# Context keys and values of layer 1 moved into the first phase of a two-layer gated attention kernel

## What is computed

```python
# layer 1, attention; context is an input, latents = layernorm(x) after layer 0
kv = jnp.concatenate([context, latents], axis=1)
q = (latents @ Wq).reshape(bsz, q_len, HEADS, HEAD_DIM).transpose(0, 2, 1, 3)
k = (kv @ Wk).reshape(bsz, kv_len, KV_HEADS, HEAD_DIM).transpose(0, 2, 1, 3)
v = (kv @ Wv).reshape(bsz, kv_len, KV_HEADS, HEAD_DIM).transpose(0, 2, 1, 3)
q, k = rms_norm(q, q_norm_w), rms_norm(k, k_norm_w)
qg = q.reshape(bsz, KV_HEADS, groups, q_len, HEAD_DIM)
probs = softmax(einsum('bhgqd,bhkd->bhgqk', qg, k) * scale)
out = einsum('bhgqk,bhkd->bhgqd', probs, v) ... @ Wo
# layer 0: k = context @ w_k.T, v = context @ w_v.T, 32 heads; codes of the
# feed-forward: idx = sum over planes p of ((qweight[p] >> shift) & 1) << p
```

## Time and profile before

| | us |
|---|---|
| median of 3 runs | 1750.46 (1750.33 to 1751.2) |
| the profiled execution | 1750.49 |
| its span, first to last instruction | 1748.7 |
| outside the span | 1.8 |
| PE busy | 1701.0 (97%) |
| PE weight loads busy | 1540.4 (88%) |
| DVE busy | 1146.8 (66%) |
| ACT busy | 856.4 (49%) |
| POOL busy | 554.3 (32%) |
| mean granted clock of PE | 0.991 |

### The profile page before, as it was taken

How to read it: one execution, slowest core, us unless ns; L and a number is a source line. 1 busy time by engine, 2 the same in 40 slices (tenths; PEclk the granted TensorE clock), 3 DMA queues, 4 the chain that set the end, 5 groups by cost and what they waited for, 6 DMA issues and landing times.

```text
span 1748.7 us, 31125 instructions
## 1 busy us (share of the span) xinstructions
PE 1701.0 (97%) x11031; PEld 1540.4 (88%) x11031; DVE 1146.8 (66%) x2064; ACT 856.4 (49%) x2254; POOL 554.3 (32%) x530
## 2 busy tenths in 40 slices
PE   6999999989999999999889999999999999999998
PEld 5999999978999999999768989898998989898987
DVE  7334443788777777778987566675756666565576
ACT  4333434444445454454425555555555555555553
POOL 4232222253222222222343333233333333232243
PEclk8999999999999999999989999999999999999999
DMA  5343434532333233332201001000100101010001
GB/s 219 146 168 144 168 144 161 184 120 84 113 105 107 94 106 112 105 105 70 88 16 37 25 25 37 12 25 22 36 24 24 36 12 42 6 36 15 1 1 48
DMA packets 62346, 132.29 MB, mean 76 GB/s; under 512 B 5200, under 2 KB 40400, under 8 KB 59216
## 3 DMA queue, kind: packets, MB, share of 16 engines
q1 hardware_dynamic: 62288, 131.52, 22.0%
HBM read 95.85 MB, written 35.65 MB: 75 GB/s over the span
## 4 chain that ended last, share of the span: by engine, by line
PE 90%; DVE 6%; ACT 1%; issue 1%; POOL 1%; DMA 0%; SPq 0%; DVEq 0%; POOLq 0%
PE bank L1611 20%; PE bank L1613 20%; PE bank L1612 19%; PE bank L1659 17%; PE bank L1955 3%; PE bank L1805 3%; PE bank L1762 3%; PE bank L1974 2%; PE bank L1750 1%; PE bank L1853 1%; PE bank L1979 1%; DVE stats L1004 1%; DVE vw_lo L1035 0%; POOL residual L562 0%; PE bank L1628 0%
## 5 line engine op out<-in xcount | busy, mean ns | idle before, releaser
L623 POOL TENSOR_TENSOR p<-p,rn 128x512 f32<-128x512 f32 x128 | 131.2, 1046 | 244.5 <-DVE rn L1487 244.5
L565 POOL TENSOR_TENSOR pr<-pr,rn 128x512 f32<-128x512 f32 x64 | 66.7, 1042 | 369.2 <-DVE rn L1234 369.2
L1611 PE MATMUL bank<-w_hi,xt_hi 128*128 (+2 forms) x512 | 177.6, 347 | 0.0
L1613 PE MATMUL bank<-w_hi,xt_lo 128*128 (+2 forms) x512 | 172.5, 337 | 0.0
L1612 PE MATMUL bank<-w_lo,xt_hi 128*128 (+2 forms) x512 | 171.3, 335 | 0.0
L1611 PE MATMUL bank<-xt_hi,w0q_hi 128*128 128x256 f32 x512 | 149.4, 292 | 0.0
L919 ACT ACTIVATE p<-bank,nb,q_r 128x256 f32<-128x256 f32 x256 | 141.3, 563 | 11.5 <-DVE nb L1483 4.8
L1612 PE MATMUL bank<-xt_lo,w0q_hi 128*128 128x256 f32 x512 | 144.0, 281 | 0.0
L1613 PE MATMUL bank<-xt_hi,w0q_lo 128*128 128x256 f32 x512 | 143.9, 281 | 0.0
L494 POOL TENSOR_TENSOR q_r<-q_ms,half 128x4 f32<-128x4 f32 x64 | 64.5, 1008 | 210.1 <-DVE q_ms L1463 210.1
L826 ACT ACTIVATE ptr<-bank 128x512 f32<-128x512 f32 x63 | 37.7, 598 | 185.9 <-PE bank L1750 185.9
(11 more groups left out here) (225 smaller groups left out, 5547.7 us busy)
## 6 DMA issues: line engine op xcount, KB each, us to landing
stage<-w SPq DMA_DIRECT2D x35, 512.0 KB, 3.3
keys_of_layer<-kout SPq DMA_DIRECT2D x16, 1024.0 KB, 4.3
values_of_layer<-vout SPq DMA_DIRECT2D x16, 1024.0 KB, 4.8
kt<-keys_of_layer SPq DMA_DIRECT2D x64, 256.0 KB, 3.1
vs<-values_of_layer SPq DMA_DIRECT2D x64, 256.0 KB, 2.8
kraw<-wk SPq DMA_DIRECT2D x16, 512.0 KB, 5.2
vraw<-wv SPq DMA_DIRECT2D x8, 1024.0 KB, 6.7
stage0q<-w SPq DMA_DIRECT2D x16, 512.0 KB, 3.8
```

Of the source, the lines that this page charges most:

```text
L565: pool.tensor_tensor(by4(pr), by4(pr), rn[:, :].unsqueeze(2).to_broadcast([P, 4, P]), ALU.mult).then_inc(norm_done, 1)
L623: pool.tensor_tensor(p1[:, half_p:half_p + 2, :], p1[:, half_p:half_p + 2, :], rn1[:, half_p:half_p + 2].unsqueeze(2).to_broadcast([P, 2, ...
L1611: nc.tensor.matmul(out_ap, l_hi, r_hi, start=(c == 0), stop=False)
L1613: op = nc.tensor.matmul(out_ap, l_lo, r_hi, start=False, stop=(c == n - 1))
```

## The change

1. In the first phase, after the eight groups of layer 0, four groups (`EG = KV // 2`) of two jobs each (k = 4, 5) make the context's keys and values of layer 1 for all 8 key/value heads by the same Strassen scheme, with the machinery of the values jobs; they are stored to DRAM (`kv1d`). Their weight sums are on DVE (`value_sums`), except those of the first group.
2. In layer 1, `keys_values` makes the latents' tile alone. The context's tile comes by DMA into a small double buffer (`kvc`), and `kv_out`, `v_low` and `k_scaled` read it there.
3. The weight codes are unpacked on DVE in the first two context groups in place of slots 1 to 7 of layer 0; `dequantise` runs once in every slot from the first on.
4. Rows of x are normalised and transposed during the context groups in place of the last group of layer 0.
5. The values' weight is split in three pieces (EARLY, MIDDLE, LAST) in place of two, and the order of the first operations differs: POOL's sums wait until three differences have been split, ACT's first evacuation of a values job comes ahead of the fourth difference.
6. `fbias` is loaded and scaled after layer 0; SP issues its DMA after the last `dequantise` and ahead of the five loads of layer 1's first weights.

```diff
         @block.sync
+            def store_context(e, half_s):
+                all_quarters(number(e, 4 + half_s))
+                for m in range(2):
+                    sp.dma_start(kv1d[2 * e + m, :, :, :]..., values_out(4 + half_s)[:, :, :, m, :])...
...
+            sp.wait_ge(wl_done, C * 2 ** LO_BITS)
+            sp.dma_start(fbias[:, :], ffn0_bias.to_broadcast([P, D])).then_inc(fbias_in, 16)
             for piece, used, count in ((2, w_lo_done[1], NG), (0, q_ps, U - 4), (1, y_ps, U - 4), (3, added, U), (4, s_ps, U)):
...
+            def load_context(t, j, held=True):
+                if held:
+                    sp.wait_ge(k1_scaled, BODY * t + j - 1)
+                sp.dma_start(kvc[:, j % 2, :], kv1d[t, :, j, :]).then_inc(kvc_in[j % 2], 16)
...
         @block.gpsimd
             weight_sums(vraw, vraw_in, vsum_done, 0, 0)
+            pool.wait_ge(t_lo_done, 7)
...
         @block.scalar
-            values_early(0)
+            values_weight(0, EARLY, 2)
             difference_hi(T2)
             first_keys(0, 0)
             first_keys(0, 1)
+            values_weight(0, MIDDLE, 5)
             difference_hi(T3)
             difference_hi(T1)
-            values_late(0)
-            difference_hi(T4)
             first_keys(1, 0)
             first_keys(1, 1)
...
+            def kv_out(count, place, loads):
                 for tile in range(2):
+                    if tile == 0:
+                        act.wait_ge(kvc_in[place % 2], 16 * loads)
+                    else:
+                        act.wait_ge(kv1_ps, count)
+                    nc.scalar.activation(v_hi[:, place, tile, :], key_value(tile, place)[:, P:2 * P], ACT.Copy)
+                    last_op = nc.scalar.activation(k_sq[:, tile, :], key_value(tile, place)[:, 0:P], ACT.Square,
                                                    accum_out=k_ss[:, tile:tile + 1])
...
         @block.vector
+            def context_projections(e):
+                values_weight_lo(SG + e, MIDDLE)
+                quarter11(e, 4)
+                quarter21(*((e - 1, 5) if e else (SG - 1, 3)))
+                values_weight_lo(SG + e, LAST)
+                quarter22(e, 4)
+                if e == 0:
+                    quantising_constants()
+                    unpack(0, "shift")
+                if e == 1:
+                    unpack(2, "shift")
+                if e == 2:
                     row_stats(0, 0)
                     row_stats(0, 1)
...
+                quarter11(e, 5)
+                quarter21(e, 4)
+                if e < EG - 1:
+                    value_sums(SG + e + 1)
+                    values_weight_lo(SG + e + 1, EARLY)
...
+                quarter22(e, 5)
+                if e == 0:
+                    unpack(0, "mask add")
+                    unpack(1, "shift mask add")
+                if e == 1:
+                    unpack(2, "mask add")
+                    unpack(3, "shift mask add")
+                if e == EG - 2:
+                    dve.wait_ge(lnw_in, 16)
+                    for b in range(3):
+                        normed_rows(0, b)
+                    row_stats(0, 2)
+                    row_stats(0, 3)
...
+                if first and j == 0:
+                    dve.wait_ge(vd_out, 16 * NG + 32 * EG)
+                    link(nc.vector.memset(wl[:, :, :], 0.0))
+                dequantise(2 * t + j // 4, j % 4, i + 1)
...
             def v_low(count, place):
                 dve.wait_ge(k1_squared, count)
+                for tile in range(2):
+                    last_op = nc.vector.tensor_tensor(v_lo[:, place, tile, :], key_value(tile, place)[:, P:2 * P],
+                                                      v_hi[:, place, tile, :].bitcast(fp32), ALU.subtract)
+                last_op.then_inc(v1_lo_done, 1)
...
         @block.tensor
+            def context_projections(e):
+                for k in (4, 5):
+                    products_early(e, k)
+                    products_last(*((e, 4) if k == 5 else (e - 1, 5) if e else (SG - 1, 3)))
+                    products_middle(e, k)
...
             def keys_values(b, parity, count):
                 wait(pe, kt1_lo_done, count - 1)
                 wait(pe, v1_lo_done, count - 1)
-                for tile, (xh, xl) in enumerate(((ct_hi, ct_lo), (xt_hi, xt_lo))):
-                    op = passes(by2(KVB[:, :])[:, tile, :],
-                                [(xh[:, c, tok(b)], xl[:, c, tok(b)], w1_hi[:, parity, 256 * c:256 * (c + 1)],
-                                  w1_lo[:, parity, 256 * c:256 * (c + 1)]) for c in range(C)])
+                op = passes(by2(KVB[:, :])[:, 1, :],
+                            [(xt_hi[:, c, tok(b)], xt_lo[:, c, tok(b)], w1_hi[:, parity, 256 * c:256 * (c + 1)],
+                              w1_lo[:, parity, 256 * c:256 * (c + 1)]) for c in range(C)])
```

More of the change, by code:

```diff
@@ L476, in _ @@
             sp.dma_start(fbias16, ffn1_bias.to_broadcast([P, D])).then_inc(fbias_in, 16)
+            for j in range(BODY):
+                slot1(KV - 1, j)
             for b in range(B):
@@ L762, in projections @@
                 part4(s, 1)
-                if last:
-                    for b in range(3):
-                        scaled_rows(b)
                 part1(s, 2)
@@ L791, in _ @@
             projections(SG - 1)
+            for e in range(EG):
+                context_projections(e)
             transposed_hi(0, 2)
             transposed_hi(0, 3)
-            quarter12(SG - 1, 3)
+            quarter12(EG - 1, 5)
             scaled_rows(5)
@@ L1263, in slot @@
                     dve.wait_ge(valid_done, 1)
-                if first and j == 1:
-                    dequantising_constants()
-                if first and (j, "middle") in UNPACK:
-                    unpack(*UNPACK[j, "middle"])
-                if last:
-                    dequantise(2 * (TL - 2) + j // 4, j % 4, BODY * (TL - 2) + 2 * j + 1)
                 inverse_sums(i + 1, 2 * (j % 4))
@@ L1697, in products_middle @@
             def products_middle(s, k):
-                job = 4 * s + k
-                ready, count = (kw_lo_done, 4 * s + k + 2) if k % 2 == 0 else (vw_lo_done, 2 * s + 2)
-                first = isinstance(s, int) and s == 0 and k == 1
-                pe.wait_ge(ready, count)
+                job = number(s, k)
+                first = isinstance(job, int) and job == 1
+                weight_ready(s, k, 2)
                 if first:
@@ L1725, in projections @@
                 first = isinstance(s, int) and s == 0
-                last = isinstance(s, int) and s == SG - 1
                 for k in range(1 if first else 0, 4):
@@ L1740, in _ @@
             projections(0)
-            with pe.Fori(1, SG - 1) as s:
+            with pe.Fori(1, SG) as s:
                 projections(s)
-            projections(SG - 1)
-            products_last(SG - 1, 3)
+            for e in range(EG):
+                context_projections(e)
+            products_last(EG - 1, 5)
             def transposed_probabilities(count):
```

397 lines of the change are left out of this document (222 added, 175 removed).

## The result

The changed kernel takes 1835.07 us (median of four runs, 1833.84 to 1837.75) against 1750.39 us (1750.12 to 1751.2) for the kernel before, a ratio of 1.0485 with a 95% interval of 1.0467 to 1.0503. The profiled execution took 1833.84 us, 83.3 more than that of before; its span is 1832.1 us, 83.4 more. The forecast was 78 more, 1828.5 us, with a range from 1806 to 1848.

What follows compares the result with a forecast made beforehand. PE is busy all the time, but a second loop through softmax is nearly as long, with 0.22 us of slack. 100 - 10 - 8 - 6 + 2 = 78 us on 1750.5 gives 1828.5 us, range 1806 to 1848.

Steps and rivals of the forecast that it cites:

- Part 1: Layer 1 slots, 12 context matmuls taken out: slot from 12.66 to 12.49 us, softmax loop binding, 10 us gained in all.
- Parts 2 and 3: First phase: 672 added matmuls cost 79.0 us, and with waits for DVE's side work and low clock 100 us longer.
- the two waits for the MIDDLE rest: First two context groups: PE idle 6.3 us, twice, while unpacking in DVE's queue delays the MIDDLE weight, 12.6 us.
- "late weight" rival: Context jobs: a 1 MB weight lands late behind the stores, 3 us for each of four groups, 1840 us; chance 0.12.
- Part 4: First operations of the kernel: product 6 of the values job starts 7.0 us earlier, gain 8 us (5 to 9).
- Part 5: Layer 0 slots: unpacking leaves, a memset and a `dequantise` come into slot 0, gain 6 us (3 to 8).
- Part 6: Transition to layer 1: SP waits for the last `dequantise` ahead of five weight loads, 2 us longer (0 to 5).
- PE-bound throughout: Whole kernel: PE stays the bound and all new waits are covered, 1.41 us gained a slot, 1725 us; chance 0.06.
- the full slots with a waiting first phase: Layer 1 slots gain all of 1.41 us, first phase waits as forecast, 1748 us, no change; chance 0.05.
- the covered unpacking: Context jobs: unpacking on DVE causes less than 2 us of wait, 1813 us; chance 0.12.
- POOL paying for `v_low`: Layer 1 slots: POOL is slowed by `v_low` with two SBUF inputs, gain only 1 us in all, 1837.5 us; chance 0.12.
- clock did not fall in layer 1: Rival: the clock falls behind waits in every layer 1 slot, 105 us lost, 1933 us; chance 0.03.

Runs made afterwards that it cites:

- Experiment 1: The kernel before with the context's tile of keys_values (12 matmuls) made only for the first count, nothing added to the first phase: 1736.45 us.
- the half: The changed kernel with 6 of 12 query matmuls ahead of the transposes and the attention output's rounded-probability matmuls first: 1759.91 us.
- experiment 5: The kernel before with the values' weight in three pieces and the changed order of the first operations: 1743.3 us.
- experiment 4: The changed kernel with SP's DMAs reordered: next values weight ahead of two loads in the first context group, fbias behind the five loads: 1823.98 us.

## Why the prediction was right, point by point

**What bounds the kernel: right.** The reading that turned the sign was the 0.22 us between POOL's end and the fifth transpose. Experiment 1 shows it on the kernel before itself.

**Part 1: right.** Forecast: slot 12.49 us, 10 us gained. Measured: 12.47 us and 12.7 us in the stage; 0.19 x 62 = 11.8 of it is the slots. The release is 0.05 us again (POOL ends at 1123.35, the weight load begins at 1123.40); from there to the next maxima are 6.28 us where 6.30 was counted. The waits are 0.50 and 0.28 us, 0.78 in all, where about 0.5 at each half and 1.2 in all were forecast. The slot does hold 1.17 us more than the 11.30 of the half, but 0.4 of that lies in rows where PE counts as busy. The price of `v_low` was also placed rightly: its context piece comes at 1122.60, when POOL's second half is running, and it is DVE that pays:

```profile
L1549 DVE TENSOR_TENSOR v_lo<-keys_values_of_context,v_hi x64: 278/918/1085, 1006.6 to 1785.9; 128x128 fp32r<-128x128 f32 x64
L1549 DVE TENSOR_TENSOR v_lo<-bank,v_hi x64: 277/278/289, 1006.8 to 1786.1; 128x128 fp32r<-128x128 f32 x64
```

(minimum, median, maximum in ns). The same subtraction of 128 columns takes 0.28 us alone, 0.92 us at the median with two SBUF inputs beside POOL, and 0.28 us with one input in PSUM; but that piece comes second, behind POOL's end (at 1123.42 in this slot), so it says nothing of what POOL would do to it. POOL's halves stay at 1.02 to 1.04 us. The piece that starts at 1122.60 ends at 1123.50, 0.15 us behind POOL's end at 1123.35. The rule of the Trainium skill, "SBUF — State Buffer", section "SBUF: two separate sides", that the pair is held for a whole instruction and the other engine fully blocks, agrees with this ending.

**Parts 2 and 3: right in kind, 5 us short.** By the start's 7.4 us (experiment 5), the phase grew by 97.8 + 7.4 = 105.2 us where 100 was forecast. Term by term: matmuls 79.0 forecast, 19.95/168 x 672 = 79.8 measured; the two waits for the MIDDLE rest 12.6 and 13.3 (6.81 + 6.46); the statistics 2.8 and 2.2; the EARLY pieces 1.5 and 1.05. Two terms were mis-sized. The clock: 4 us forecast as half of a four-microsecond stretch behind each of two waits. By the windows it is 2.4 and 1.5 us there, and 1.6 us more behind a wait of 2.74 us for which I had charged nothing, 5.5 in all. And that wait itself, 2.7 us: it was my "late weight" rival, at one group and not at four. In the first context group SP issues the load behind a store and two other loads (from 335.20 to 337.45) and it lands after 10.9 us; in the next two groups it stands behind a store alone and lands after 6.8 and 7.4. These sum to 104.6. The clock's part is no fixed price: by experiment 4 the same first phase took up to 2.6 us longer in other executions, so the forecast was 5 to 8 us short.

**Part 4: right.** Product 6 was forecast at about 26.6 and starts at 26.01; 8 us forecast, 7.4 measured in experiment 5. The 1 us counted for the clock did not come: the first four microseconds ran at about 0.67 in place of 0.50, but PE then waits 0.62 us for ACT at 31.21.

**Part 5: right by less than forecast.** -4.6 in place of -6. From slot 1 to slot 9 the change gained 8.8 us (61.5 in place of the 70.3 of the earlier trace rows), but slot 0 lasts 9.23 us where it lasted 5.69, because the maxima of slot 1 stand on DVE behind a memset of 1.76 us and a `dequantise`. I had left 2 us for both; they cost 3.5.

**Part 6: the sum right, by two errors.** 2 us forecast, 2.9 measured. But the wait for the five loads is 6.1 us, not the 2 that I charged, and the rest of the transition became 3.7 us shorter than in the kernel before, as experiment 4 shows (71.9 us in place of 75.5 with the DMA out of the way). For most of this there is a cause that I had overlooked: the context's tiles of the first two slots were made in the transition, and one of them alone was worth 1.5 us in experiment 1. I had listed the moved wait in SP's queue and not followed it to `ot_hi`, which is queued behind ACT's wait.

**The rivals.** PE-bound throughout, the full slots with a waiting first phase, the covered unpacking, and POOL paying for `v_low` are out by the stages above. The clock did not fall in layer 1: 1.00 from 1030 to 1790 us, although PE waits twice in every slot, with four transposes between. Nor did it in the tail, on which that rival rested: there the changed kernel waits 1.49 us at 1797.29 and runs at 1.00 in the eight microseconds from 1795.

**What was luck.** The total is 5 us off because the first phase came out 5.8 us, the transition 0.9 and layer 0 1.4 above the forecast and layer 1 2.7 us below it; the transition's own term was right only because two errors of about 4 us cancelled.

## What to carry to other kernels

A busy engine is a bound only as far as the next loop is shorter than its own work. Before matmuls are taken out of a loop, subtract, in one iteration, the end of the last step of each other chain from the start of the instruction that takes it: here the slack was 0.22 us against 1.41 us to be removed, and nearly everything removed turned into a wait.

Work taken out of a balanced loop has to come with a new order. Moving half of an independent product ahead of the waiting transposes brought 75 us, moving all of it cost 9, and in the unchanged kernel the same move brought nothing.

Side work for a queue that feeds the bound engine goes in pieces no longer than the slack of each place: the same 23 us of unpacking cost about 17 us in two clumps (13.3 of waiting, 3.9 of low clock) and nothing to be seen in eleven pieces.

## What the runs showed of the hardware

The granted clock behind a wait of two to seven microseconds was low for a time that differed between executions of the same work. Behind the wait of 6.46 us in the changed kernel the stretches of two microseconds ran at 0.50 and 0.76; behind the same wait in `dma_order_after` they ran at 0.50, 0.50 and 0.52. Behind the wait of 2.74 us the clock was 0.60 over four microseconds. Behind the wait of 2.17 us it was 1.00 in the changed kernel and 0.62 and 0.52 in `dma_order_after`. What decides between the two no run here shows. In layer 1, with two waits of under 1 us in every slot of 12.47 us, it stayed at 1.00.

A load of 1 MB took 10.9 us to land when issued behind two loads and a store, and 7.6 us when issued ahead of the two loads; five loads of 512 KB took 7.2 us at the median behind the bias and 5.4 us ahead of it.

A DVE subtraction of 128 columns with two SBUF inputs took 0.92 us at the median beside POOL's normalisation, and 0.28 us at the shortest.
